# An attention and mixture-of-experts block: three score banks in the last batch, tile 0 routed earlier, high parts unmasked, roots turned at once

## The reference

```
x = x + layernorm(attention(layernorm(x)))      # 16 heads of 8, softmax over 256 keys, biases on q, k, v, o
x = x + layernorm(experts(layernorm(x)))

experts(x):
  scores = sigmoid(x @ gate_w.T)                # 32 experts in 8 groups of 4
  sc = scores + e_bias
  group  = sum of the 2 best sc in a group; the 4 best groups stay, the others' sc become 0
  chosen = the 6 best experts by that; weight w_e = 2.5 * score_e / sum of the chosen scores
  h_e    = relu(x @ up_w[e].T)**2 * w_e         # 64 wide
  result = sum_e h_e @ down_w[e].T + relu(x @ shared_up.T)**2 @ shared_down.T
```

## Time and profile before

| | |
|---|---|
| median of 3 executions | 515.81 us |
| profiled execution, its own time | 516.76 us |
| its span, first to last instruction | 514.9 us |
| mean granted TensorE clock | 0.948 |
| TensorE matmul busy | 467.5 us, 91% |
| VectorE busy | 399.8 us, 78% |
| ScalarE busy | 362.2 us, 70% |
| GpSimd busy | 227.9 us, 44% |

### The profile page before, as it was taken

The page is one execution under the profiler, slowest core; times in us unless marked ns, Lnnn a source line. Parts: engine busy times, 40 slices in busy tenths (PEclk is TensorE's granted clock), DMA queues, the critical chain, the costliest instruction groups (busy, mean ns, idle before and its releaser), DMA issues.

```text
span 514.9 us, 10734 instructions
## 1 busy us (share of the span) xinstructions
PE 467.5 (91%) x3352; PEld 269.1 (52%) x3352; DVE 399.8 (78%) x1031; ACT 362.2 (70%) x723; POOL 227.9 (44%) x546
## 2 busy tenths in 40 slices
PE   2458999999999999998899899999999999999994
PEld 1213444444444444454346566666666676766662
DVE  3678788899999989989826769597886869597453
ACT  3415788877888978887847476868868687866551
POOL 6054233325434635230103644839385674716251
PEclk9555899999999999999979899999999999999998
DMA  6544244454344444330024244435354445536421
GB/s 201 163 136 131 87 124 125 141 149 134 124 129 134 144 141 128 116 97 2 5 87 164 87 164 164 168 114 199 94 171 158 162 164 152 202 99 202 130 109 41
DMA packets 48280, 67.47 MB, mean 131 GB/s; under 512 B 3808, under 2 KB 34784, under 8 KB 48224
## 3 DMA queue, kind: packets, MB, share of 16 engines
q1 hardware_dynamic: 48224, 66.78, 41.3%
HBM read 51.17 MB, written 15.20 MB: 129 GB/s over the span
## 4 chain that ended last, share of the span: by engine, by line
PE 71%; DVE 15%; issue 8%; ACT 4%; POOL 1%; DMA 0%; POOLq 0%; DVEq 0%; ACTq 0%
PE pO L1304 9%; PE pY L1387 8%; PE pS L1246 8%; PE pS L1387 8%; DVE mneg L920 7%; PE pS L1371 6%; PE pS L1373 6%; PE pS L1372 6%; PE pS L1252 2%; PE pX L1231 2%; PE pY L1321 2%; PE pX L1234 2%; PE pY L1333 1%; DVE q_rest L900 1%; PE pX L1226 1%
## 5 line engine op out<-in xcount | busy, mean ns | idle before, releaser
L920 DVE TENSOR_REDUCE mneg<-pS 128x2 f32<-128x512 f32 x256 | 162.7, 685 | 17.2 <-PE pS L1246 16.5
L702 ACT ACTIVATE probs<-pS 128x512 f32<-128x512 f32 x256 | 142.5, 595 | 26.5 <-PE pS L1252 24.8
L1246 PE MATMUL pS<-qk 48*128 48x256 bf16 x512 | 88.9, 289 | 20.4 <-DVE mneg L920 10.9
L1252 PE MATMUL pS<-qk 51*128 51x256 bf16 x512 | 89.9, 281 | 1.7 <-ACT probs L702 1.5
L788 ACT ACTIVATE h_ring<-r 128x512 f32<-128x512 f32 x104 | 65.0, 625 | 35.1 <-DVE r L1090 26.1
L1371 PE MATMUL pS<-qk,up_hi 128*128 128x512 f32 x144 | 88.8, 617 | 0.0
L1304 PE MATMUL pO<-probs,vv 128*32 128x256 f32 x1024 | 74.0, 396 | 0.0
L1246 PEld LDWEIGHTS pS<-qk 48*128 48x128 bf16 x512 | 33.5, 96 | 73.8 <-DVE mneg L920 48.7
L1090 DVE SCALAR_TENSOR_TENSOR r<-pS,probs 128x512 f32<-128x512 f32 x64 | 43.4, 687 | 23.0 <-PE pS L1373 22.5
L1090 DVE SCALAR_TENSOR_TENSOR r<-pS,c_ring 128x512 f32<-128x512 f32 x64 | 44.0, 688 | 17.0 <-PE pS L1373 14.6
L1373 PE MATMUL pS<-qk,up_lo 128*128 128x512 f32 x144 | 57.1, 397 | 0.0
(11 more groups left out here) (190 smaller groups left out, 823.3 us busy)
## 6 DMA issues: line engine op xcount, KB each, us to landing
c_ring<-c_scratch SPq DMA_DIRECT2D x32, 512.0 KB, 4.0
probs<-c_scratch SPq DMA_DIRECT2D x32, 512.0 KB, 3.8
qk<-qk_scratch SPq DMA_DIRECT2D x64, 192.0 KB
qk_scratch<-q_parts SPq DMA_DIRECT2D x16, 192.0 KB, 2.3
qk_scratch<-k_parts SPq DMA_DIRECT2D x16, 192.0 KB, 2.1
qk_scratch<-q_parts SPq DMA_DIRECT2D x16, 128.0 KB, 2.2
qk_scratch<-k_parts SPq DMA_DIRECT2D x16, 128.0 KB, 2.0
out_x<-probs SPq DMA_DIRECT2D x7, 256.0 KB, 4.8
```

The lines of the kernel that those rows point to most:

```text
L702: nc.scalar.activation(probs[j][:, hh], pS2[n % S2_RING][:, :, :], ACT.Exp, scale=SCALE).then_inc(exp_done, 1)
L920: nc.vector.tensor_reduce(mneg[u % 2][:, :, hh, k], pS1[n % S1_RING][:, :].rearrange("p (a s) -> p a s", a=TH), AX.X, ALU.max, negate=True ...
L1246: return mm(pS1[n % S1_RING][:, T * th:T * (th + 1)], qp[slot][rows, k, P * th:P * (th + 1)], kp[slot][rows, k, :], start=True, stop=True)
L1252: return mm(pS2[n % S2_RING][:, sh], kp[slot][rows, k, P * sh:P * (sh + 1)], qp[slot][rows, k, :], start=True, stop=True)
```

## The change

In the last batch the scores by key use three banks, the third being `pS1[2]` (`s2_bank`, `pLate`). Two up products of tile 0 move into it: the first after pair 5, the second between the two last groups of outputs. Tile 0's logits move from batch 13 to batch 12, and its routing steps to other places; `high_x(0)` moves from step 8 of the last batch to step 4 of batch 14, and the subtraction for x is done at step 13 of batch 14. The high parts are no longer masked: ScalarE writes the fp32r value from the whole value, and the low part is what that leaves. For the up weights this subtraction moves from VectorE to GpSimd (`low_up`, in batches 5 to 9), for x it stays on VectorE (`low_x`). The roots of a tile, 128 tokens x (32 experts x 4), are laid out so that one transpose of 128x128 turns them, and `cT` is 128x128 instead of 32x512. In tiles 1 to 7 `high_x` moves from block 15 to block 8, the subtraction from 14 to 12.

```diff
+S2_LATE, N_LATE = 3, H * (NB - 1)
-ROUTE_FIRST = {(NB - 3, 12): 0, (NB - 3, 14): 1, (NB - 2, 8): 2, (NB - 2, 10): 3, (NB - 2, 12): 4, (NB - 1, 1): 5,
-               (NB - 1, 3): 6, (NB - 1, 5): 7}
-FIRST_ROOT = (NB - 2, 12)
+ROUTE_FIRST = {(NB - 3, 2): 0, (NB - 3, 4): 1, (NB - 3, 12): 2, (NB - 2, 8): 3, (NB - 2, 12): 4, (NB - 2, 15): 5,
+               (NB - 1, 0): 6, (NB - 1, 2): 7}
+FIRST_ROOT = (NB - 2, 10)
...
+        pLate = [pS2[0], pS2[1], pS1[2][:, :].rearrange("p (a t) -> p a t", a=TH)]
+        def s2_bank(n):
+            return pS2[n % S2_RING] if n < N_LATE else pLate[(n - N_LATE) % S2_LATE]
...
+            def low_up(c):
+                pool.wait_ge(whi_done, c + 1)
+                blocks = slice(CUT * c, min(CUT * (c + 1), FBLK))
+                nc.gpsimd.tensor_tensor(up_lo[:, blocks].rearrange("p a b -> p (a b)"), up_in[c],
+                                        up_hi[:, blocks].rearrange("p a b -> p (a b)").bitcast(F32),
+                                        ALU.subtract).then_inc(wlo_done, 1)
...
                     if u // 2 + 2 < NB:
                         part2(u // 2 + 2)
                         part3(nc.gpsimd, pool.wait_ge, u // 2 + 2)
+
+                    if CUT_BATCH + 2 <= u // 2 < CUT_BATCH + 2 + NCUT:
+                        low_up(u // 2 - CUT_BATCH - 2)
...
             def high_up(c):
-                act.wait_ge(wcut_done, c + 1)
+                act.wait_ge(up_loaded[c], 16)
...
-                    if s == 8 and last:
+                    if s == 4 and b == NB - 2:
                         high_x(0)
...
-                    if s == 11 and CUT_BATCH <= b < CUT_BATCH + NCUT:
-                        cut_up(b - CUT_BATCH)
-
-                    if last and s == 0:
-                        cut_x(0)
+                    if b == NB - 2 and s == 13:
+                        low_x(0)
...
-                for c in range(C4):
-                    ins = tr(pX[0:E, P * c:P * (c + 1)], root_c[:, c], idf[:, :])
-                ins.then_inc(cT_done, 1)
+                tr(pX[:, 0:P], root_c[:, :, :].rearrange("p e c -> p (e c)"), idf[:, :]).then_inc(cT_done, 1)
...
                     if j == 5:
                         outputs(b, 0, 1)
                         outputs(b, 1, 0)
+                        if last:
+                            pe.wait_ge(max_done, H * NB)
+                            up_block(0, 0)
...
             for sh in range(TH):
                 outputs(NB - 1, 2, sh)
-
-            pe.wait_ge(max_done, H * NB)
-            pe.wait_ge(exp_done, TH * NBLK * NB)
+            up_block(0, 1)
+            for sh in range(TH):
+                outputs(NB - 1, 3, sh)
+
             for i in range(NTILE):
                 for k in range(FBLK):
                     n = FBLK * i + k
-                    up_block(i, k)
+                    if n >= 2:
+                        up_block(i, k)
                     downs(n)
-                    if i == 0 and k == 0:
-                        for sh in range(TH):
-                            outputs(NB - 1, 3, sh)
```

More of the change, by code:

```diff
@@ L192, in block_kernel @@
         w_sum, w_root = sb("w_sum", [P, C4]), sb("w_root", [P, C4])
[L193 removed]
+        comb, root = (sb(n, [P, C4, E]) for n in ("comb", "root"))
+        root_c = sb("root_c", [P, E, C4])
+        root_by_c = root_c[:, :, :].rearrange("p e c -> p c e")
         root_v, root_h = (sb(n, [P, C4, E]) for n in ("root_v", "root_h"))
         root_t = comb
[L196 removed]
+        cT = sb("cT", [P, P])
         c_ring = ([sb(f"c_ring{i}", [P, CGROUP, TILE]) for i in range(2)]
@@ L840, in _ @@
                         keep_xT(0)
-                    if s == 7 and b == NB - 3:
+                    if s == 0 and b == NB - 3:
                         exp_logits(0)
@@ L1251, in key_scores @@
                 rows = slice(HALF * KEY_HEADS[i], HALF * KEY_HEADS[i] + DIFF_ROWS)
-                return mm(pS2[n % S2_RING][:, sh], kp[slot][rows, k, P * sh:P * (sh + 1)], qp[slot][rows, k, :],
+                return mm(s2_bank(n)[:, sh], kp[slot][rows, k, P * sh:P * (sh + 1)], qp[slot][rows, k, :],
                           start=True, stop=True)
```

77 lines of the change are left out of this document (24 added, 53 removed).

## The result

| | before | after |
|---|---|---|
| median, 4 executions each on one chip | 515.72 us (515.42 to 517.17) | 509.04 us (508.40 to 510.52) |
| profiled execution, its own time | 516.76 us | 508.58 us |
| its span | 514.9 us | 506.8 us |

The ratio of the times is 0.987, with a 95% interval of 0.984 to 0.990. The change saves 6.7 us where 8.0 were forecast.

What follows compares the result with a forecast made beforehand. TensorE, 91% busy, was taken as the bound, losing time to waits and the lower clock. Terms -4.0 + 0.5 - 1.9 - 0.7 - 1.9 = -8.0 us took 515.81 to 507.8 us, range 503.8 to 512.3.

Steps and rivals of the forecast that it cites:

- (b): Batches 12 to 14: tile 0's routing and the copy of x's high part moved earlier cost +0.5 us.
- (e): Tiles 1 to 7: masking of x gone and its copies earlier, worth 0; tile 0's stop of 1.82 us stays.
- (a): Batches 4 to 9: high parts unmasked, low parts of the up weights on GpSimd, -4.0 us.
- (c): Last batch: roots of tile 0 ready sooner, so TensorE transposes them earlier, -1.9 us.
- (d): Expert tiles: one transpose of the roots instead of four, -0.7 us in tile 0 and -1.9 in seven tiles.
- cover of 3.1 us for GpSimd: Batches 5 to 9: slack before TensorE takes GpSimd's split maxima, hiding the new subtraction, so nothing is added.
- the prediction's own sign for it: Batch 13: the prediction is wrong if VectorE's routing makes TensorE wait more than 1.5 us.
- third rival: Batch 13: moved routing puts VectorE behind, all of it on TensorE's path; 511.8 us, chance 0.09.
- first rival: Last batch: the clock doesn't fall, another 1.6 us saved; 506.2 us, chance 0.23.
- The second: Batches 4 to 8: ScalarE's copy and normalisations also limit, so (a) gives 1.5 instead of 4.0; 510.3 us, chance 0.19.
- The fourth: Batches 5 to 9: GpSimd's subtraction holds VectorE's instructions, 10.8 us come back; 518.6 us, chance 0.04.
- The fifth: Batches and last batch: other waits keep their length, no change; within 1.5 us of 515.8, chance 0.05.

Runs made afterwards that it cites:

- the repeated kernel: The changed kernel itself, unaltered, measured again beside the follow-up experiments: 509.23 us (505.87 to 510.58, 6 executions).
- e3: The changed kernel with two banks instead of three for the scores in the last batch: 513.03 us (511.99 to 513.16).
- e4: The changed kernel with four transposes of the roots a tile again, old layout, copy and write: 512.67 us (509.07 to 513.83).

## Why the prediction was nearly right, and which step failed

The time fell into the range, and 509.0 is 1.2 us above the forecast. Between the profiled executions the sum of the stretches is -8.13 us, where the terms gave -8.0. That agreement is partly luck: (b) was missed by +1.2, and of (e) -1.6 and of the last batch some tenths are falls of the clock that one execution has and another has not. By the medians, -6.7, the forecast took 1.3 us too much. By the work that they name, (a), (c), (d) and (e) came out nearly as worked out.

**(a)** Forecast -4.0, measured -3.8 over the six intervals and -3.87 at the mark of batch 12. The terms match one by one: batch 4 -0.78 for 0.69, batches 5 and 7 -1.06 and -1.05 for 1.06 each, batch 6 -0.47 for 0.6, batch 8 -0.44 for 0.3; only batch 9 gave nothing (-0.01 for 0.3). Some 0.55, 0.55 and 0.72 us above 13.45 remain in batches 6, 8 and 9, which carry the normalisations; no run takes these out. The cover of 3.1 us for GpSimd held, and held twice the work.

**(b)** Forecast +0.5, measured +1.72 and, in the repeated kernel, 29.97 - 26.83 = +3.14. This is the step that failed, and the prediction's own sign for it was met: TensorE waits 1.20 + 0.38 = 1.58 us for VectorE's row maxima in batch 13, more than 1.5. The mechanism, VectorE behind ahead of row maxima, was named in this term and, at full weight, as third rival. It took VectorE to be behind there from the wait of 0.54 us at 240.51, but that row lies behind the mark of batch 13 (236.45): VectorE was behind in batch 14, and kept up in batch 13 until the routing came. The routing moved out of batch 14 is time won there: the three waits for row maxima before (0.16, 0.36 and 0.54 us) are gone. Without falls the two batches take 14.57 (with the filling) and 12.51, together 27.1 against 26.8: the +0.5 is right for the moved work by itself, within 0.3 us. What was missing is that the clock falls to half behind stops of 0.44, 1.20 and 0.38 us in a row; with the middle one filled it didn't. All seven profiled executions with the early routing had a fall in batch 13 or 14, and of the seven without it only the one that kept the early copy of x had one. I had looked at the clock in the last batch alone, where it fell already.

**(c) and tile 0's part of (d)** Forecast -2.6, with a fall of the clock as long as before. With a fall, but of 3.4 us instead of 6.8, the stretch is 17.40 instead of 19.88, -2.48; with the weights alone a fall as short made this stretch 0.46 us shorter by the same instructions, so up to that much of the 2.48 is the clock. Of the work: the roots' wait went from 1.15 to 0.24 us. They are turned at 254.49 instead of 258.40, 3.91 us sooner, of which 2.15 were won ahead of the mark of batch 14: 1.76 in the last batch, for a forecast of 1.9. Without the fall it is 15.49, -4.4, where first rival and forecast together give -4.2. The third bank's part of it is 0.4 us. The two moved products are nothing that the trace shows.

**(d)** Forecast -1.9 for seven tiles, measured -1.65, and with the four transposes put back exactly 1.65 more. The gain is 0.24 us a tile instead of 0.27. The strided write that no row of before showed costs 0.1 us, off TensorE's path. All its executions, kernel after (ns: min, median, max), and then the kernel before:

```profile
L1031 DVE SCALAR_TENSOR_TENSOR root_c<-e_left,root x8: 370/376/407, 251.9 to 453.7; 128x128 f32<-128x128 f32 x8
```

```profile
L1019 DVE SCALAR_TENSOR_TENSOR root_c<-e_left,root x8: 277/279/285, 256.0 to 461.4; 128x128 f32<-128x128 f32 x8
```

**(e)** Forecast 0, with the stop unchanged. The stop is longer, 2.20 us, its cause was named wrongly (it is the wait ahead of the statistics, not the routing), and the stretch 1.85 us shorter, because in that execution no fall of the clock came behind the stop. In the repeated kernel it has one, as before, and takes 41.98, against 42.22. So 0 was right for the work within 0.24 us, and -1.6 of the profiled difference was luck of the execution.

**The rivals.** The first (no fall in the last batch, 506.2) is a matter of the execution, not of the kernel: it held in the repeated kernel, and its 1.6 us were measured as 1.9. What decides between the two is not shown. The second (the cut only one of two limits) is refuted by the intervals of batches 4, 5 and 7 and by the weights alone. The third found the right place with the wrong currency: it priced 4 us of VectorE's time in batch 13, and most of the lost time is TensorE's own clock. The fourth is refuted: no row maximum got longer, with the subtractions or with twice as many. Its condition never came up, since no VectorE instruction with two SBUF inputs ran beside them in batches 5 to 9. Elsewhere it shows: the 128x128 instruction at 281.70, which reads two inputs from SBUF, took 1.34 us beside a GpSimd subtraction of 1.29 us that began at 281.61, as one did before. By the rule of the Trainium skill, GPSIMD Engine Reference, section Specifications, that was to be expected there and not for row maxima, which read PSUM; the trace agrees, with 0.29 us at best against 1.34 us for the one kind (L1026) and 683 ns throughout for the other. The fifth is refuted.

By medians the account is less clean than by marks. Falls come in some executions and not in others, each worth 1.4 to 2.9 us, and the mean granted clock of each execution on record goes with its time. The median of e3 lies 3.8 us and more above those of the kernel after, where the marks give the third bank 0.4 to 0.7; that of e4 3.4 us and more, where they give the transposes 1.9. Up to batch 14 the instructions and stops of both are those of the kernel after. The traces show half clock for longer in batch 13; why all executions of e3 and six of eight of e4 were long, they don't show.

## What to carry to other kernels

Price a wait of the matmul engine with the clock behind it: a row of short stops can cost more again in the microseconds in which the engine is busy (here 1.5 to 2.9 us beside 1.1), so when work is moved, count the stops that it gathers into one place, not only their sum. Work that is moved from an idle place to an earlier one should go where the feeding engines have slack, batch by batch, and secondary work (statistics, copies for later) belongs behind the instruction that the matmul engine waits for. Judge parts of a change by marks inside the traces and by repeated executions; a median mixes them with falls of the clock that come in some executions only.

## What the runs showed of the hardware

- The granted clock is not decided by the program alone. The same kernel with the same stops had it at half in 228 to 231 and 255 to 259 us in one execution, and in 230 to 234, 244 to 247 and 285 to 288 in another.
- Each fall between 60 and 495 us came behind stops and lasted 3 to 7 us; those in batch 13 began 0.3 to 2.2 us after TensorE had gone on from the stop of 1.20 us. In one traced execution two matmuls without use in a stop left no fall there: the batch went from 16.0 or more to 14.6 us. Stops of 0.58 and 0.32 us in batch 14 had a fall behind them in six of seven executions, 13.85 to 13.90 us, and none in the seventh, 12.51. No single stop ahead of the fall in batch 13 was longer than 1.20 us.
- A mean granted clock says little. It was 0.957 in the fastest profiled execution of all (502.64 us) and 0.948 before, in both mostly for the stretch from 13 us on at half clock, which left no mark on the batches: batch 1 has its mark at 69.83 us before and at 69.75 in the kernel after, which had no such stretch.
- A VectorE instruction that writes 128x128 floats with a stride of 16 bytes takes 376 ns instead of 279. GpSimd's two-input subtraction of 128x512 takes 1.27 to 1.29 us, and VectorE's reductions from PSUM beside it are not slowed (683 ns with and without).
